# A prefetch hint at the head of each engine's loop: an attention stage and six local-attention layers on one Trainium2 core

## What is computed

```python
x = _layernorm(x + _L0_attn_ref(x, Wqa, Wqb, Wkva, Wkvb, Wout, bout))
# _L0_ffn_ref, DEPTH = 6, on x of (4, 1024, 128):
for i in range(DEPTH):
    x = attn_layer(shift_tokens(x), Wqkv[i], q_scale[i], k_scale[i], Wo[i]) + x
    x = ffn_layer(shift_tokens(x), ln_g[i], ln_b[i], W1[i], b1[i], W2[i], b2[i]) + x
x = _layernorm(x_before + x)

def attn_layer(x, Wqkv, qs, ksc, Wo):
    q, k, v = split(x @ Wqkv)                 # 128 -> 3 * 1024, 16 heads of 64
    q, k = rotary(l2norm(q) * qs), rotary(l2norm(k) * ksc)
    return local_attention(q, k, v) @ Wo      # softmax over 64 keys, window 32

def ffn_layer(x, g, bln, W1, b1, W2, b2):     # 128 -> 2 * 341 -> 128
    a, gate = split((layernorm(x) * g + bln) @ W1 + b1)
    return a * gelu(gate) @ W2 + b2
```

## Time and profile before

| | |
|---|---|
| median of three runs | 4710.56 us (4701.91 to 4711.07) |
| the profiled execution | 4716.59 us, of which 4714.8 us from the first to the last instruction (its span) |
| busy share of the span | PE 88%, DVE 62%, POOL 59%, ACT 56% |
| mean granted TensorE clock | 0.957 of full speed |
| jumps back in the local layers | 22 on each of five engines, from 1222 to 4451 us on PE |
| jumps back in the attention stage | 2 on each of four engines |

### The profile page before, as it was taken

One profiled execution on the slowest core, in us unless ns is written; L12 is line 12 of the kernel. 1 busy time (PEld: TensorE's weight loads), 2 busy tenths in 40 slices (PEclk: granted clock), 3 DMA queues, 4 the chain that ended last, 5 costly groups with the idle time before them and its releaser, 6 DMA issues. The chain is left out here.

```text
span 4714.8 us, 163642 instructions
## 1 busy us (share of the span) xinstructions
PE 4147.4 (88%) x67078; PEld 2777.6 (59%) x67078; DVE 2916.1 (62%) x4217; ACT 2622.4 (56%) x4417; POOL 2799.6 (59%) x3584
## 2 busy tenths in 40 slices
PE   5878788689999999999999999999999999999994
PEld 2434344356666666666666666666666666666663
DVE  5565656566666666666666666666666666666664
ACT  2535354446556565665656655656566555665662
POOL 0000000177777777777777777777777777777771
PEclk9979788899999999999999999999999999999997
DMA  0000000112222122222222222222222222222223
GB/s 27 3 15 2 16 16 3 42 45 58 69 71 72 51 69 65 72 57 64 65 69 64 56 66 69 77 53 69 65 72 56 65 65 69 64 56 65 69 66 79
DMA packets 284548, 258.85 MB, mean 55 GB/s; under 512 B 122872, under 2 KB 258509, under 8 KB 271149
## 3 DMA queue, kind: packets, MB, share of 16 engines
q1 hardware_dynamic: 283820, 248.14, 19.7%
HBM read 117.63 MB, written 29.77 MB: 31 GB/s over the span
## 5 line engine op out<-in xcount | busy, mean ns | idle before, releaser
L785 DVE TENSOR_TENSOR products<-bank_d,table 128x1024 f32<-128x1024 f32 x772 | 938.1, 1216 | 716.5 <-ACT sq L612 711.8
L908 POOL TENSOR_TENSOR products<-products 128x2048 f32<-128x2048 f32 x192 | 870.4, 4533 | 263.1 <-DVE products L785 263.1
L411 PE MATMUL bank_d<-w_qkv,xT 128*128 128x512 f32 x1544 | 805.6, 625 | 25.2 <-DVE products L785 14.2
L612 ACT ACTIVATE sq<-bank_d 128x512 f32<-128x512 f32 x772 | 467.8, 606 | 484.8 <-PE bank_d L411 474.6
L945 POOL TENSOR_TENSOR qk_rot<-products,rnorm 128x2048 f32<-128x2048 f32 x192 | 695.4, 3622 | 15.0 <-POOL rnorm L927 14.6
L783 DVE TENSOR_REDUCE ss<-sq 128x16 f32<-128x1024 f32 x386 | 468.7, 1214 | 240.3 <-ACT sq L612 240.3
L952 POOL TENSOR_TENSOR prob<-prob,inv_sum 128x1024 f32<-128x1024 f32 x192 | 365.1, 1902 | 407.3 <-DVE inv_sum L765 407.3
L872 POOL MEMSET ident<- 128x128 f32 x1 | 0.2, 204 | 914.6 <-POOLq L1062 914.6
L1489 DVE TENSOR_REDUCE part_max<-s_max 128x1 f32<-128x512 f32 (+3 forms) x768 | 398.3, 554 | 150.7 <-PE s_max L1238 101.2
L457 PE MATMUL bank_a<-ident,qk_rot 128*128 128x128 f32 x3072 | 412.6, 290 | 69.6 <-issue 64.0
L457 PEld LDWEIGHTS bank_a<-ident,qk_rot 128*128 128x128 f32 x3072 | 366.9, 149 | 150.4 <-issue 103.0
(11 more groups left out here) (168 smaller groups left out, 7551.9 us busy)
## 6 DMA issues: line engine op xcount, KB each, us to landing
v_back<-v SPq DMA_DIRECT2D x96, 768.0 KB, 5.5
w_qkv<-in_Wqkv_dram SPq DMA_DIRECT2D x25, 1024.0 KB, 5.0
v_back<-v SPq DMA_DIRECT2D x192, 128.0 KB, 5.5
w_qkv<-in_Wqkv_dram SPq DMA_DIRECT2D x25, 512.0 KB, 5.5
xs<-x_layers SPq DMA_DIRECT2D x194, 64.0 KB, 2.1
w_o<-in_Wo_dram SPq DMA_DIRECT2D x24, 512.0 KB, 6.0
xr<-x_layers SPq DMA_DIRECT2D x96, 128.0 KB, 2.2
x<-x SPq DMA_DIRECT2D x96, 128.0 KB, 1.8
```

What stands on the lines that cost most here:

```text
L411: nc.tensor.matmul(bank[:, :], xT[:, P * a:P * (a + 1)], w_qkv[:, col:col + 512], start=True, stop=True).then_inc(d_filled if i < 8 else a ...
L612: nc.scalar.activation(sq[j % 2][:, 8 * c:8 * c + 8, :], bank_d[slot][:, :].rearrange("p (h d) -> p h d", d=DH), ACT.Square).then_inc(squa ...
L785: nc.vector.tensor_tensor(products[:, a, head:head + 8, :, :].rearrange("p h r (o d) -> p h r o d", o=2), bank[:, :].rearrange("p (h r d) ...
L908: link(nc.gpsimd.tensor_tensor(products[:, a, :, 0, :], products[:, a, :, 0, :], products[:, a, :, 1, :], ALU.add))
```

## The change

Both loops are opened by another call. In place of `eng.Fori(1, N)` stands `nc.Fori(1, N, engines=[eng.engine], hint_back_edge=True)`: the same loop with one instruction more, a `BRANCH_PREFETCH_HINT` at the head of the body, which names the engine's `COMPARE_BRANCH` at the end of that body. Nothing else differs: no operation, wait, buffer or transfer is added, removed or moved.

```diff
@@ rounds, local layers
             for p in range(POS):
                 step_fn(Step(0, p))
-            with eng.Fori(1, ROUNDS) as f:
+            with nc.Fori(1, ROUNDS, engines=[eng.engine], hint_back_edge=True) as f:
                 for p in range(POS):
                     step_fn(Step(f, p))
@@ batches, attention stage
             body(0)
-            with eng.Fori(1, BATCH) as b:
+            with nc.Fori(1, BATCH, engines=[eng.engine], hint_back_edge=True) as b:
                 body(b)
```

## The result

The changed kernel takes **4737.91 us** (median of 5 runs, 4728.98 to 4740.4) against 4708.4 us (4701.91 to 4711.07, 5 runs) for the kernel before: ratio **1.0058**, 95% interval [1.0044, 1.0072]. It is slower by some 27 us by that ratio (29.5 us between these two medians), where 107 us less were forecast. The profiled execution took 4738.34 us, 21.8 more than the one of before.

A forecast was written before the change was run, and what follows sets the result against it. PE's idle time and clock were taken to bound the kernel. Stall 57 + clock 49 + attention stage 2 - hints 1 = 107 us saved, so 4710.6 - 107 = 4604 us, range 4583 to 4635; 4583 to 4706 held some 8 in 10.

The forecast's parts named there:

- what the hint buys on PE: PE's branch at each local-layer jump: 2.6 of 2.9 us idle saved, 22 times, 57 us; bounds 0 and 2.9.
- The first rival: At PE's branch: hint works only when the engine enters the last piece; 4690 to 4702 us; chance 0.22.
- The part on the change: 23 hints on each of five engines, 3 on each of four; 0.05 us each on PE, 1 us in all.
- The hint's own cost: PE's sequencer in the local rounds: 0.05 us, 22 times, 1 us; nothing on POOL, DVE and SP.
- The clock: PE's lower clock behind each local-layer jump: all regained, 22 x 2.2 = 49 us; bounds 0 and 49.
- ACT's stall: ACT's code fetch after its branch, 2.5 us at one jump, hidden behind PE; taken as gone with the hint.
- attention stage: PE's two taken branches in the attention stage: 1 us saved at each, 2 us, from 0 to 4.
- The second rival: At local-layer jumps: stall goes, but ACT's fetch isn't covered or the clock falls; 60 us saved, 4651; chance 0.12.
- The third: On PE the hint does nothing, forgotten over four steps or its piece overwritten; 4711 us within 3; chance 0.09.
- The fourth: At the loop's head: hint fetches too early, a piece is fetched again; 33 to 64 us slower, 4744; chance 0.07.

The follow-up runs named there:

- 142: Kernel before, no hints, with PE's local loop starting at slot 142 of the 256 instruction places taken for one code packet; ratio 1.0043.
- slot 188: Changed kernel, all hints, with PE's local loop starting at place 188 of 256 in a code packet; 4873.08 us, ratio 1.0371 to before.
- a pair: Two kernels with PE's local loop at the same place in its code packet, one with all hints, one without; hints worth 66 to 143 us.
- slot 111: PE's local loop starting at place 111 of 256 in a code packet; ratio to before 0.9992 with all hints, 1.0141 without.
- slot 20: PE's local loop starting at place 20 of 256 in a code packet; ratio to before 0.9987 with all hints, 1.0315 without.
- slot 100: PE's local loop starting at place 100 of 256 in a code packet; 4700.27 us (ratio 0.998 to before) with all hints, 4788.5 us (1.016) without.
- 28: PE's local loop starting at place 28 of 256 in a code packet; ratio to before 0.9922 with all hints, 1.0105 without.

## Why the prediction was wrong

The forecast of 4604 us and its range up to 4706 both missed 4738, and slower had a chance of 0.08.

- **The step that failed** is "what the hint buys on PE", from which 57 us and then 49 us of clock were taken. It bounded the gain by 0 and 2.9 us a jump and took 2.6, on the assumption that the target's piece is asked for together with the last piece. The branch stayed at 3.5 us. The runs put in its place: the hint only turns the next fetch that PE makes anyway, and that one comes when PE is well inside the last piece; with the branch 13 to 60 instructions into it the target's packet still starts 1.0 us after the branch began, at 148 to 239 it starts 1.3 to 3.2 us ahead. The row that should have warned was the one I used for the sum, the last piece entered 0.3 us ahead of the branch.
- **The first rival** had this reason, a hint that helps only from the entry into the last piece, and with it the sentence that it is useless wherever a branch stands near a boundary. Even its 7 us didn't come: the branch shortened by 147 ns in the median, 22 x 0.147 = 3 us, and without hints at the same place (142) it is as short, 3476 ns. In its strict form it fell too, at slot 188.
- **What no term held** is the shift. The part on the change counted the time of the added instructions and not their place. Yet the stall ahead of the branch had been read at L411, right behind L518, and a piece boundary stood at that very instruction. Two instructions more in front of it put it inside L518, ahead of ACT's copy and of the transposes that covered the branch. That cost 20 us by the kernel without hints (1.0043), of which its rows show 76.9 - 64.0 = 12.9 at L457 and 20.8 - 19.4 = 1.4 ahead of the branch; the rest is not placed.
- **The hint's own cost** was taken as 1 us; 7 to 13 were measured, cause open. Together with the shift, 27 to 33 us, against the 27 measured.
- **The clock** term hung on the first: the pause behind the jump got longer, not shorter, and PEclk fell as before. Between the members of a pair the wait at L457 differs by 53 to 67 us, the time by 66 (slot 111) to 143 us (slot 20), so how much the clock gives back was not isolated. Its premise held where the branch is short: the clock then stays at 1.00 behind all 22 jumps.
- **ACT's stall** went, as forecast, and was hidden behind PE, as forecast. The **attention stage** gave 0.7 us between its branches, of 2 (0 to 4). There too the hint took a packet away, 14 on q8 from one of PE's branches to the next where it was 15; how far into its piece that branch stands was not worked out.
- **The second rival** wasn't put to the test by this kernel. **The third**, that the hint is forgotten, fell at slot 100. **The fourth**, slower by fetching too early, had the right sign and the wrong mechanism: the page has 580 packets on q8 over the span (581 before), 22 in a round as before.

In the Trainium skill, "Runtime: NRT & Kernel Launch", section "Instruction fetch mechanics", it says that crossing a 16 KiB boundary is mostly hidden. Most boundaries of this body are; those that aren't cost what this page is about: 23.9 us at L518 and 27.8 us in 23 pieces at L498 in the profile after, 3.6 us a round at L476 at slot 100. The same section's rule that prefetch is purely sequential was the third rival's ground; it holds without a hint, down to the packet for the piece behind the loop, and not with one and the branch far into its piece, since the target's packet then starts 3.2 and 3.1 us ahead of the branch at slots 100 and 111.

## What to carry to other kernels

When a change adds or removes even one instruction in a long loop body, work out where the piece boundaries of each engine's code fall before and after, and which queued work lies between the last boundary and the branch: here two instructions were worth 0.4%, and other placements of the same code, without any hint, from 0.4% to 3.2% more than before. A prefetch hint is worth its place: with the branch 156 instructions into its piece the hints gave 82 us, with it at 13 they gave none and cost some 10. In these runs the packets of the kernel without hints told it in advance: the hint helped where the loop made one packet a round more than its body has pieces, and not where the two were equal. So place the loop first and hint then, and try several places, since the best for the branch can put another boundary among dense small matmuls, or a fetch behind a large load.

## What the runs showed of the hardware that I had not expected

- A `BRANCH_PREFETCH_HINT` takes 31 to 42 ns in the median on the five engines. It survives a body of 5248 instructions and some 150 us, and shortens PE's taken branch from 3.6 us to 448 ns.
- It doesn't do so where the branch is 13, 23 or 60 instructions past a boundary (3.5 us), does so for the most part at 148 (1.15 us) and 156 (0.5 us in the median, 1.6 at most), and fully at 228 and 239.
- It replaces a fetch and adds none: 21 packets a round with hints and 22 without at slots 20, 28, 100 and 111, 22 in both where the branch stands 11 or 13 into its piece.
- On ACT, with a body of 348 instructions, the hint ended the fetching: no packet on q14 in the local rounds, where there were 5 a round. The time didn't change by it (0.9994 with the hints of the four other engines alone).
- Two instructions of shift, without a hint, cost 20 us of 4700; fourteen, 57 us; slot 20 without a hint 3.2%.
- A boundary costs 1 us in every round at one place (L498), nothing visible at others, and 3.6 us in 19 of 22 rounds at slot 100. At slots 100 and 20 the late packets are the ones behind a large load, round by round (above), and the packet starts as the load's own are done. No run here took those loads away, so that they are the cause is argued and not shown; for L498 there is no such sign.
